# Attention and mixture of experts on one core: weight loads one step earlier, beta added batch by batch, packing of experts in four parts

## The chip, the cores and the metric

The kernel runs on one core of a Trainium2 chip. The metric is the device time of one execution in microseconds (us). Engines are named as the profile does: PE is TensorE, DVE is VectorE, ACT is ScalarE, POOL is GpSimd, SP is SyncE, which here only issues transfers.

## The reference

The input is x, 32 batches of 256 tokens of 128 numbers. Everything is float32.

```
xn  = layernorm(x)                                   # without gamma and beta
out = x + attention(xn) + experts(xn)

attention(t): q, k, v = split(t @ w_qkv), 16 heads of 8
              a = softmax(causal(q k^T / sqrt(8))) v
              layernorm(a @ w_proj + b_proj + t) * gamma + beta
experts(t):   p = softmax(t @ Wr^T), 8 experts, the best 2 of each token
              sum over those: p_e * (gelu(t @ W1[e] + b1[e]) @ W2[e] + b2[e])
```

## The kernel before

All of the work is written out by engine; an engine runs its own list in order, and semaphores tie the lists together. There are four stages.

1. x is loaded and normalised; the router's logits are computed, and each token gets two places (slots) among the rows of its experts.
2. A loop of steps does the attention. In step s batch s is projected to q and k (PROJECT), the row maxima of batch s-1 are found (MAXIMA), batch s-2 goes through scores and exponentials (SOFT), batch s-3 through the rest up to the projection and the statistics of the second layernorm (FINISH), and batch s-4 gets gamma and is added to the residual (LAST). The list `USES` sets, for all engines, the order of the pieces of work inside a step: m0 to m11 are the products whose maxima VectorE takes (L1192 and L1196 on TensorE, L966 on VectorE), s0 to s5 the scores (L1178, L1182) with their exponentials on ScalarE (L687) and causal masks on POOL (L601), o0 and o1 the products with v (L1213), then transposes (oT, onT), the projection (proj) and the transposed maxima (shift). Steps 1 to 3 and 24 to 35 are written out; between them most engines run a loop with two steps in its body. POOL's steps are all written out.
3. Experts: 72 tiles of 256 slots, each gathered, multiplied with the two matrices of its expert and scattered.
4. The two results of each token are added to the residual and stored.

What the change touches stands in the second stage:

- **Weights of the experts.** W1 and W2 come in eight pieces of 512 KB through two buffers. SP loads piece i with `load_piece` (L424); ScalarE copies it to float16 (`high_piece`, L691, behind the copy of v, L704), and VectorE stores the difference (`low_piece`, L1036, behind the statistics of proj, L993 to L1002). `pieces(s)` says which piece a step splits: pieces 0 to 6 in steps 24 to 30, piece 7 in step 32. Pieces 0 and 1 are loaded before the loop. Piece i from 2 on is loaded at the start of the step that splits it, ahead of that step's store of q and k (L460) in SP's queue; the loads of q and k by heads (L446, L447) and of the maxima (L481) follow.
- **Beta.** `add_beta` on POOL (L579) adds beta to the residual x_all, eight tiles of 128 tokens in one instruction. Tiles 0 to 31 are done before the loop, the others in steps 5, 7, 9 and 11.
- **Order on POOL in a step.** Indirect sends of normalised rows to their slots (`send_tile`, L592, two DMAs per tile; two tiles in a step, from step 24 on three in every even one), then add_beta where the step has one, then the mask of s0, the add of the normed batch to x_all (`add_normed`, L607), a power (L613), the residual with the bias (L621), and the masks of s1 to s5.
- **Gamma.** `last` on VectorE (L1009), a pair of instructions per step, behind the maximum m11.
- **Packing of experts.** `pack_experts` on VectorE (L939 to L953), 16 operations each waiting for the one before, finds the expert of each tile and packs the numbers for the loops of stage 3. It stands at the end of step 3 (FINISH), behind proj's statistics and ahead of the next step's m0.

## Time and profile before

| | |
|---|---|
| median of 3 runs | 832.76 us (831.69 to 836.01) |
| the profiled execution | 832.92 us, of which 831.2 are the span |
| mean granted clock | 0.953 |
| PE busy | 695.6 us, 84% of the span |
| DVE busy | 663.3 us, 80% |
| ACT busy | 548.3 us, 66% |
| POOL busy | 552.3 us, 66% |
| chain that ended last | PE 65%, DVE 11%, DMA 7%, ACT 7%, issue 4%, SP's queue 3%, POOL 2% |

The span is from the first to the last instruction. The granted clock is TensorE's, as a share of 2.4 GHz; its other level is 1.2 GHz. An engine is busy while an instruction of it runs; the share of the whole span is a mean over the four stages. A row of a timeline has the start in us from the span's start, the duration in us (with "x5", from the start of the first to the end of the last of five merged ones), the engine, the line, the operation, out<-in, shapes, and in brackets the idle time before it with what ended it.

### The profile page before, as it was taken

What the parts mean: (1) busy time and instruction counts of PE and PEld (TensorE: products, weight loads), DVE (VectorE), ACT (ScalarE), POOL (GpSimd) and SP (SyncE); (2) the same over time, 40 slices, a digit from 0 to 9 for tenths busy, and PEclk for the clock granted to TensorE, in tenths of its full rate; (3) what the DMA queues carried; (4) which work ended last, traced back from release to release, by engine and by line L of the source; (5) the groups of instructions that cost most, each with busy time, mean ns of one, the idle gap of its engine ahead of it and who ended that gap; (6) DMA issues with size and microseconds to landing.
All of it is one profiled execution on the core that took longest, in us unless ns stands there. A gap on an engine that the chain in (4) does not pass through costs nothing.

```text
span 831.2 us, 24989 instructions
## 1 busy us (share of the span) xinstructions
PE 695.6 (84%) x7877; PEld 516.5 (62%) x7878; DVE 663.3 (80%) x1550; ACT 548.3 (66%) x1107; POOL 552.3 (66%) x611
## 2 busy tenths in 40 slices
PE   2766989898899999999878888669999999999800
PEld 1543656565666666666656555338988889888700
DVE  5878988889898898989988886537888888888644
ACT  4812656666576767767667665538989999999700
POOL 8522768877787888878768676616666667667700
PEclk9998999999999999999999999859999999999955
DMA  9692223232323232333253342102222222222189
GB/s 263 241 304 70 92 82 99 84 102 84 103 82 110 93 104 92 108 105 96 81 158 110 104 135 65 29 13 77 89 81 87 80 87 85 83 78 89 51 276 336
DMA packets 113313, 93.66 MB, mean 113 GB/s; under 512 B 16618, under 2 KB 97650, under 8 KB 113268
## 3 DMA queue, kind: packets, MB, share of 16 engines
q1 hardware_dynamic: 95508, 70.26, 27.4%
q0 software_dynamic: 8704, 18.17, 6.1%
q10 hardware_dynamic: 9056, 4.66, 1.9%
q8 instruction: 25, 0.41, 0.2%
q14 instruction: 20, 0.16, 0.1%
HBM read 43.85 MB, written 48.93 MB: 112 GB/s over the span
## 4 chain that ended last, share of the span: by engine, by line
PE 65%; DVE 11%; DMA 7%; ACT 7%; issue 4%; SPq 3%; POOL 2%; ACTq 0%; POOLq 0%; DVEq 0%
PE wide L1324 11%; PE bank_head L1213 7%; PE wide L1178 6%; PE bank_head L1315 5%; PE bank_maxB L1315 5%; PE bank_maxA L1192 5%; PE bank_maxB L1192 4%; DMA xn_rows<-parts_dram 3%; PE bank_misc L1238 3%; DMA pieces_f<-in_w 3%; PE wide L1182 3%; PE bank_maxB L1196 3%; PE bank_maxA L1196 3%; DVE y L1009 2%; SPq L481 2%
## 5 line engine op out<-in xcount | busy, mean ns | idle before, releaser
L653 POOL DMA_INDIRECT parts_dram<-o_T,dest x144 | 160.5, 1115 | 76.6 <-issue 47.9
L687 ACT ACTIVATE probs<-wide 128x1024 f32<-128x1024 f32 x192 | 188.7, 1021 | 32.8 <-PE wide L1178 19.2
L601 POOL TENSOR_SCALAR_AFFINE_SELECT probs<-probs 128x512 f32<-128x512 f32 (+1 forms) x192 | 152.2, 804 | 83.9 <-ACT probs L687 83.1
L592 POOL DMA_INDIRECT x_slots<-xn_rows,slot_i x128 | 127.1, 993 | 37.6 <-issue 36.5
L966 DVE TENSOR_REDUCE shift<-bank_maxA 128x2 f32<-128x512 f32 (+1 forms) x192 | 132.2, 689 | 13.8 <-PE bank_maxA L1196 10.1
L966 DVE TENSOR_REDUCE shift<-bank_maxB 128x2 f32<-128x512 f32 (+1 forms) x192 | 131.7, 686 | 7.8 <-PE bank_maxB L1196 4.1
L731 ACT ACTIVATE probs<-wide,b_all 128x256 f32<-128x256 f32 x288 | 121.2, 477 | 16.9 <-PE wide L1324 11.0
L1324 PE MATMUL wide<-xgT_raw,xnT 128*128 128x256 f16 x864 | 109.2, 277 | 6.6 <-DVE xgT_raw L1074 6.6
L1057 DVE TENSOR_TENSOR probs<-probs 128x512 f16<-128x512 f32 x144 | 99.8, 693 | 5.4 <-ACT probs L737 1.1
L1213 PE MATMUL bank_head<-probs,v_aug 128*32 128x256 f32 (+1 forms) x2048 | 98.8, 334 | 6.4 <-POOL probs L601 6.3
L1192 PE MATMUL bank_maxA<-k_cat,q_diag 128*128 128x128 f16 (+1 forms) x512 | 76.0, 251 | 19.5 <-DVE shift L966 17.9
L1324 PEld LDWEIGHTS wide<-xgT_raw,xnT 128*128 x864 | 78.7, 99 | 19.4 <-issue 7.6
L1213 PEld LDWEIGHTS bank_head<-probs,v_aug 128*32 128x32 f32 x2048 | 59.3, 111 | 49.5 <-issue 16.8
L1178 PE MATMUL wide<-q_diag,k_cat 128*128 128x512 f16 x256 | 77.5, 386 | 3.3 <-DMA q_diag<-shift_T 3.0
L1192 PE MATMUL bank_maxB<-k_cat,q_diag 128*128 128x256 f16 (+1 forms) x512 | 75.5, 251 | 0.5 <-DVE shift L966 0.2
L711 ACT ACTIVATE o_T<-bank_head 128x512 f32<-128x512 f32 x64 | 38.2, 597 | 54.5 <-PE bank_head L1213 52.0
L1192 PEld LDWEIGHTS bank_maxA<-k_cat,q_diag 128*128 128x128 f16 x512 | 38.7, 98 | 45.5 <-DVE shift L966 31.9
L1192 PEld LDWEIGHTS bank_maxB<-k_cat,q_diag 128*128 128x128 f16 x512 | 42.9, 99 | 31.2 <-DVE shift L966 11.0
L1196 PE MATMUL bank_maxA<-mask,ident 128*128 128x256 f16 (+1 forms) x192 | 60.4, 314 | 0.0
L1196 PE MATMUL bank_maxB<-mask,ident 128*128 128x256 f16 (+1 forms) x192 | 60.3, 314 | 0.0
L1315 PE MATMUL bank_head<-xnT,probs 128*128 x864 | 56.1, 222 | 0.0
L1315 PE MATMUL bank_maxB<-xnT,probs 128*128 x864 | 55.1, 220 | 0.2 <-DVE probs L1057 0.2
(178 smaller groups left out, 1263.9 us busy)
## 6 DMA issues: line engine op xcount, KB each, us to landing
qk_rows<-split SPq DMA_DIRECT2D x32, 512.0 KB
x_slots<-fill SPq DMA_DIRECT2D x16, 598.5 KB, 7.7
fill<-x_slots SPq DMA_DIRECT2D x72, 133.0 KB
q_diag<-qk_rows SPq DMA_DIRECT2D x256, 32.0 KB, 1.8
k_cat<-qk_rows SPq DMA_DIRECT2D x64, 128.0 KB, 2.1
xn_rows<-parts_dram SPq DMA_DIRECT2D x8, 1024.0 KB, 11.7
x_all<-in_x SPq DMA_DIRECT2D x8, 512.0 KB, 8.2
pieces_f<-in_w SPq DMA_DIRECT2D x8, 512.0 KB, 4.3
```

The lines of the kernel that those rows point to most:

```text
L592: pool.indirect_dma_start(out=x_slots, out_offset=bass.IndirectOffsetOnAxis(ap=slot_i[:, t, c:c + 1], axis=0), in_=xn_rows[:, t, :], in_of ...
L601: pool.affine_select(out=part, in_=part, compare_op=ALU.is_ge, fill=0.0, base=0, pattern=[[0, n], [1, P]], channel_multiplier=-1).then_inc ...
L653: pool.indirect_dma_start(out=parts_dram, out_offset=bass.IndirectOffsetOnAxis(ap=dest[:, of, t:t + 1].bitcast(U32), axis=0), in_=y[:, of ...
L687: act.activation(probs[:, u, :], ps[:, :], ACT.Exp, scale=SCALE).then_inc(empty, 1)
L731: act.activation(hT[:, par, c, :], wide[par][:, S * c:S * (c + 1)], ACT.Gelu, bias=b1_all[:, bass.ds(e, 1), c:c + 1].rearrange("p a b -> p ...
L966: V.tensor_reduce(dst, ps[:, :].rearrange("p (j k) -> p j k", j=nh), axis=AX.X, op=ALU.max, negate=True).then_inc(empty, 1)
L1178: last = M(ps[:, 512 * h2:512 * (h2 + 1)], keys[:, gs[0], :], q_diag[:, par, gs[0], 2 * h2:2 * h2 + 2, :], start=True, stop=True)
L1192: M(ps[:, keys * n_:keys * (n_ + 1)], q_diag[:, 1 - par, g, j, P * qt:P * (qt + 1)], k_cat[:, 1 - par, g, 0:keys], start=(n_ == 0), stop=F ...
L1196: M(dst, ident16[:, :], mask16[:, :].rearrange("p (o k) -> p o k", o=1).to_broadcast([P, nh, P]), start=False, stop=True, skip_group_check ...
L1213: last = M(dst, v_aug[:, of, kt, J * g + j, :], p_, start=(kt == 0), stop=(kt == 1), skip_group_check=True)
L1315: last = M(results[:, D * t:D * (t + 1)], hT_parts[:, par, hp, c, P * t:P * (t + 1)], w2_parts[:, wp_, bass.ds(e_2, 1), c, :].rearrange("p ...
L1324: last = M(wide[par][:, S * c:S * (c + 1)], w1_parts[:, wp_, bass.ds(e_1, 1), P * c:P * (c + 1)].rearrange("p a d -> p (a d)"), xgT[:, par ...
```

## The change

Three edits, with one more that one of them needs.

SP loads piece i+1 at the start of the step that splits piece i, from piece 1 on, after a wait for the split of piece i-1, whose buffer it takes. Piece 7 thus goes out in step 30. `add_beta` takes a first tile and a number of tiles; before the loop nothing changes, and in the loop one batch (two tiles) is added in each of steps 5 to 20. `pack_experts` has four parts, at the ends of steps 4, 5, 6 and 7: the three operations that find the experts, then four, four and two of the ten packing operations, and with the last part the three closing ones. As these steps differ, VectorE's loop begins with step 8 instead of step 4, and steps 4 to 7 are written out for it.

```diff
-        def steps(eng, step, after=((), ()), first_tile=None, written_out=False):
+        def steps(eng, step, after=((), ()), first_tile=None, written_out=False, in_loop=STAGES - 1):
...
-            first_whole = STAGES - 1 if not written_out else TAIL
+            first_whole = in_loop if not written_out else TAIL
...
                 for i in pieces(s):
-                    if i >= 2:
-                        sp.wait_ge(piece_low, i - 1)
-                        load_piece(i)
+                    if 1 <= i < PIECES - 1:
+                        sp.wait_ge(piece_low, i)
+                        load_piece(i + 1)
...
-            def add_beta(c):
-                tiles_ = slice(NT // BETA_PARTS * c, NT // BETA_PARTS * (c + 1))
-                pool.tensor_tensor(x_all[:, tiles_, :], x_all[:, tiles_, :],
-                                   beta_bc[:, :].rearrange("p (o d) -> p o d", o=1).to_broadcast([P, NT // BETA_PARTS, D]),
-                                   ALU.add).then_inc(res_ready if c == BETA_PARTS // 2 - 1 else offset_ready, 1)
+            def add_beta(begin, count):
+                mine = x_all[:, begin:begin + count, :]
+                pool.tensor_tensor(mine, mine, beta_bc[:, :].rearrange("p (o d) -> p o d", o=1).to_broadcast([P, count, D]),
+                                   ALU.add).then_inc(res_ready if begin + count == NT // 2 else offset_ready, 1)
...
-                    if what == "m0" and s in (5, 7, 9, 11):
-                        add_beta(BETA_PARTS // 2 + (s - 5) // 2)
+                    if what == "m0" and 5 <= s < 5 + B // 2:
+                        add_beta(QT * (B // 2 + s - 5), QT)
...
-            def pack_experts():
-
-                dve.wait_ge(slots_filled, 256)
-                then_pack(V.tensor_tensor(past[:, :, :], tile_start[:, :].rearrange("p (t o) -> p t o", o=1).to_broadcast([P, NS, E]),
-                                     over_tiles(ends[:, :], NS), ALU.is_ge))
-                then_pack(V.tensor_reduce(expert[:, :], past[:, :, :], axis=AX.X, op=ALU.add))
-                then_pack(V.tensor_scalar(padded_experts[:, 2:2 + NS], expert[:, :], float(E - 1), None, ALU.min))
-                for j in range(FIELDS):
+            def pack_experts(part):
+
+                if part == 0:
+                    dve.wait_ge(slots_filled, 256)
+                    then_pack(V.tensor_tensor(past[:, :, :], tile_start[:, :].rearrange("p (t o) -> p t o", o=1).to_broadcast([P, NS, E]),
+                                              over_tiles(ends[:, :], NS), ALU.is_ge))
+                    then_pack(V.tensor_reduce(expert[:, :], past[:, :, :], axis=AX.X, op=ALU.add))
+                    then_pack(V.tensor_scalar(padded_experts[:, 2:2 + NS], expert[:, :], float(E - 1), None, ALU.min))
+                for j in (range(0, 0), range(0, 4), range(4, 8), range(8, FIELDS))[part]:
...
+                if part == 3:
+                    then_pack(V.tensor_copy(packed_i[:, :, :], packed[:, :, :]))
...
-                if isinstance(s, int) and s == FINISH:
-                    pack_experts()
+                if isinstance(s, int) and FINISH < s <= FINISH + 4:
+                    pack_experts(s - FINISH - 1)
...
-            steps(dve, step, after=((), (places,)), first_tile=lambda: tile(0, 0, None))
+            steps(dve, step, in_loop=FINISH + 5, after=((), (places,)), first_tile=lambda: tile(0, 0, None))
```

How it moves the work shows in the lists of three engines. In the changed kernel the lines below L311 of the file are off by one here and there (L592 is L591, L1002 is L1003).

SP, from the end of step 24 to the start of step 26, before (L424 is the load of a piece, L460 the store of q and k):

```order
L481 DMA q_diag<-shift_T 1x4x256 x4
L460 DMA qk_rows<-split 128x2x1024
L446 DMA q_diag<-qk_rows 32x2x256 x4
L447 DMA k_cat<-qk_rows 128x2x256
L446 DMA q_diag<-qk_rows 32x2x256 x4
L447 DMA k_cat<-qk_rows 128x2x256
L481 DMA q_diag<-shift_T 1x4x256 x4
L424 DMA pieces_f<-in_w 128x2x512
L460 DMA qk_rows<-split 128x2x1024
```

and in the changed kernel:

```order
L481 DMA q_diag<-shift_T 1x4x256 x4
L424 DMA pieces_f<-in_w 128x2x512
L460 DMA qk_rows<-split 128x2x1024
L446 DMA q_diag<-qk_rows 32x2x256 x4
L447 DMA k_cat<-qk_rows 128x2x256
L446 DMA q_diag<-qk_rows 32x2x256 x4
L447 DMA k_cat<-qk_rows 128x2x256
L481 DMA q_diag<-shift_T 1x4x256 x4
L424 DMA pieces_f<-in_w 128x2x512
```

The load of piece 2 now stands in front of step 25's store of q and k instead of step 26's, and each later load has moved in the same way.

POOL, step 5 and the sends of step 6, before (L579 adds beta, L607 the normed batch):

```order
L592 DMA x_slots<-xn_rows,slot_i 18432x133 x4
L579 TENSOR_TENSOR x_all<-x_all,beta_bc 128x1024
L601 AFFINE_SELECT probs<-probs 128x4x128
L607 TENSOR_TENSOR x_all<-x_all,y2 128x256
L613 TENSOR_TENSOR rstd2<-mv2,half 128x2
L621 TENSOR_TENSOR xpb<-xn_rows,bproj_bc 128x256
L601 AFFINE_SELECT probs<-probs 128x4x128
L601 AFFINE_SELECT probs<-probs 128x1024
L601 AFFINE_SELECT probs<-probs 128x4x128 x2
L601 AFFINE_SELECT probs<-probs 128x1024
L592 DMA x_slots<-xn_rows,slot_i 18432x133 x4
L601 AFFINE_SELECT probs<-probs 128x4x128
```

and in the changed kernel, from the last masks of step 5:

```order
L600 AFFINE_SELECT probs<-probs 128x4x128 x2
L600 AFFINE_SELECT probs<-probs 128x1024
L591 DMA x_slots<-xn_rows,slot_i 18432x133 x4
L579 TENSOR_TENSOR x_all<-x_all,beta_bc 128x256
L600 AFFINE_SELECT probs<-probs 128x4x128
L606 TENSOR_TENSOR x_all<-x_all,y2 128x256
```

The add is a quarter of its size and now stands behind the sends of step 6 too, and so on to step 20.

VectorE, where the packing stood, from the end of step 3 to the loop, before (L1002 closes the statistics, L939 begins the packing):

```order
L1002 TENSOR_SCALAR mv<-mv 128x2
L939 TENSOR_TENSOR fill<-tile_start,ends 128x576
L941 TENSOR_REDUCE expert<-fill 128x72
L942 TENSOR_SCALAR padded_experts<-expert 128x72
L947 COPY packed<-padded_experts 128x10
L949 SCALAR_TENSOR_TENSOR packed<-padded_experts,packed 128x10 x4
L947 COPY packed<-padded_experts 128x10
L949 SCALAR_TENSOR_TENSOR packed<-padded_experts,packed 128x10 x4
L951 CAST packed_i<-packed 128x20
L952 TENSOR_SCALAR packed_i<-packed_i 128x10
L953 TENSOR_TENSOR packed_i<-packed_i 128x10
```

and in the changed kernel, the end of step 4 and the start of step 5 (L967 takes the maxima, L983 splits q and k):

```order
L1010 SCALAR_TENSOR_TENSOR y<-x,mv,gamma_bc 128x128 x2
L994 TENSOR_TENSOR x<-bank_misc,xpb 128x256
L997 BN_STATS st<-x 128x6 x2
L1001 BN_AGGR mv<-st 128x2 x2
L1003 TENSOR_SCALAR mv<-mv 128x2
L939 TENSOR_TENSOR fill<-tile_start,ends 128x576
L941 TENSOR_REDUCE expert<-fill 128x72
L942 TENSOR_SCALAR padded_experts<-expert 128x72
L967 TENSOR_REDUCE shift<-bank_maxA 128x4
L967 TENSOR_REDUCE shift<-bank_maxB 128x2
L983 TENSOR_TENSOR split<-bank_misc,split 128x2x256
```

Three of the sixteen operations are left at one place, a step later than before; the other thirteen follow the statistics of steps 5, 6 and 7.

## Rows read from the trace of the kernel before

**Rows 1.** Stretches: us from:to, length, busy time of each engine (instructions), granted clock, DMA share, GB/s.

```profile
90.11:106.77 16.66, 14.63 (x171) 9.36 (x159) 14.67 (x40) 9.33 (x13) 12.66 (x15) 1.00 0.29 93
106.77:121.33 14.56, 14.28 (x134) 9.12 (x137) 11.72 (x27) 8.83 (x13) 8.09 (x11) 0.88 0.23 75
121.33:149.97 28.64, 27.09 (x304) 17.80 (x296) 24.27 (x52) 18.76 (x28) 23.53 (x28) 1.00 0.31 98
149.97:224.19 74.22, 66.99 (x748) 44.86 (x740) 66.23 (x131) 46.95 (x70) 61.35 (x70) 1.00 0.28 91
237.51:370.84 133.33, 133.20 (x1488) 89.00 (x1480) 118.41 (x260) 93.17 (x140) 106.55 (x131) 1.00 0.31 100
384.05:400.66 16.61, 13.92 (x169) 9.45 (x158) 15.55 (x28) 10.27 (x15) 14.30 (x17) 1.00 0.33 99
400.66:414.25 13.59, 13.14 (x152) 8.95 (x148) 12.82 (x28) 10.26 (x15) 9.64 (x11) 1.00 0.28 89
414.25:493.81 79.56, 67.11 (x748) 45.51 (x741) 66.53 (x137) 51.25 (x75) 60.34 (x72) 1.00 0.40 124
107.20:110.60 3.40, 3.21 (x18) 1.73 (x16) 2.35 (x5) 0.96 (x2) 0.25 (x1) 0.65 0.47 174
514.10:518.10 4.00, 3.98 (x19) 2.83 (x20) 1.94 (x4) 2.25 (x3) 3.90 (x6) 0.57 0.00 0
```

**Rows 2.** Timeline of VectorE, the packing and the maximum behind it.

```profile
100.81 0.75 DVE L939 TENSOR_TENSOR fill<-tile_start,ends 128x576 f32<-128x576 f32 x1
...
102.62 0.17 DVE L947 COPY packed<-padded_experts 128x10 f32<-128x10 f32 x1
...
105.57 0.69 DVE L966 TENSOR_REDUCE shift<-bank_maxA 128x4 f32<-128x512 f32 x1 [0.25 <-DVE packed_i L953]
```

**Rows 3.** Timeline of TensorE, the first product of step 4 that waits.

```profile
106.32 0.39 PE L1192 MATMUL bank_maxA<-k_cat,q_diag 128*128 128x256 f16 x2 [1.90 <-DVE shift L966]
```

**Rows 4.** Timelines of VectorE and TensorE, the split in step 25 and step 26's wait.

```profile
411.92 1.21 DVE L1036 TENSOR_TENSOR xnT<-pieces_f,xnT 128x1024 f16<-128x1024 f32 x1
...
415.78 0.39 PE L1192 MATMUL bank_maxA<-k_cat,q_diag 128*128 128x256 f16 x2 [0.20 <-DVE shift L966]
```

**Rows 5.** Timeline of POOL in step 23, a clean one.

```profile
373.07 0.96 POOL L592 DMA_INDIRECT x_slots<-xn_rows,slot_i  x1 [0.30 <-issue]
374.88 0.63 POOL L601 TENSOR_SCALAR_AFFINE_SELECT probs<-probs 128x512 f32<-128x512 f32 x1 [0.86 <-ACT probs L687]
375.49 0.71 POOL L607 TENSOR_TENSOR x_all<-x_all,y 128x256 f32<-128x256 f32 x1
...
380.22 0.73 POOL L601 TENSOR_SCALAR_AFFINE_SELECT probs<-probs 128x512 f32<-128x512 f32 x1 [0.28 <-ACT probs L687]
```

**Rows 6.** Timeline of POOL in step 7: the add of beta and the masks.

```profile
153.18 2.38 POOL L579 TENSOR_TENSOR x_all<-x_all,beta_bc 128x1024 f32<-128x1024 f32 x1
...
158.17 3.93 POOL L601 TENSOR_SCALAR_AFFINE_SELECT probs<-probs 128x512 f32<-128x512 f32 x5
```

**Rows 7.** Timeline of VectorE, the gamma pair in steps 7, 23 and 24.

```profile
158.98 3.27 DVE L1009 SCALAR_TENSOR_TENSOR y<-x,mv,gamma_bc 128x128 f32<-128x128 f32 x2
...
379.85 0.60 DVE L1009 SCALAR_TENSOR_TENSOR y<-x,mv,gamma_bc 128x128 f32<-128x128 f32 x2
...
393.07 3.71 DVE L1009 SCALAR_TENSOR_TENSOR y<-x,mv,gamma_bc 128x128 f32<-128x128 f32 x2
```

**Rows 8.** Waits: who waited for what, us in total, times, longest.

```profile
ACT xnT L691 <- DMA pieces_f<-in_w: 16.4, 6, 3.6
```

**Rows 9.** DMA issues: number, KB each, median us from issue to landing.

```profile
pieces_f<-in_w SPq DMA_DIRECT2D x8, 512.0 KB, 4.3
```

**Rows 10.** Timeline of POOL, masks of step 24 and first send of step 26.

```profile
392.49 3.88 POOL L601 TENSOR_SCALAR_AFFINE_SELECT probs<-probs 128x512 f32<-128x512 f32 x5
...
412.16 1.88 POOL L592 DMA_INDIRECT x_slots<-xn_rows,slot_i  x1 [0.17 <-issue]
```

**Rows 11.** Timeline of TensorE in step 32.

```profile
514.12 0.80 PE L1182 MATMUL wide<-q_diag,k_cat 128*128 128x512 f16 x2 [2.51 <-ACT probs L687]
```

More of the change, by code:

```diff
@@ L587, in _ @@
             for c in range(BETA_PARTS // 2):
-                add_beta(c)
+                add_beta(NT // BETA_PARTS * c, NT // BETA_PARTS)
             def send_tile(t):
@@ L950, in pack_experts @@
                                                     op0=ALU.mult, op1=ALU.add))
-                then_pack(V.tensor_copy(packed_i[:, :, :], packed[:, :, :]))
-                then_pack(V.tensor_scalar(packed_i[:, 1, :], packed_i[:, 1, :], BITS * FIELDS // 2, None, ALU.logical_shift_left))
-                then_pack(V.tensor_tensor(packed_i[:, 0, :], packed_i[:, 0, :], packed_i[:, 1, :], ALU.bitwise_or))
-                assert packing_count == EXPERTS_PACKED, packing_count
+                if part == 3:
+                    then_pack(V.tensor_copy(packed_i[:, :, :], packed[:, :, :]))
+                    then_pack(V.tensor_scalar(packed_i[:, 1, :], packed_i[:, 1, :], BITS * FIELDS // 2, None, ALU.logical_shift_left))
+                    then_pack(V.tensor_tensor(packed_i[:, 0, :], packed_i[:, 0, :], packed_i[:, 1, :], ALU.bitwise_or))
+                    assert packing_count == EXPERTS_PACKED, packing_count
             FAR = 1e38
@@ L1127, in _ @@
             picks()
-            steps(dve, step, after=((), (places,)), first_tile=lambda: tile(0, 0, None))
+            steps(dve, step, in_loop=FINISH + 5, after=((), (places,)), first_tile=lambda: tile(0, 0, None))
             tiles(dve, tile, load=False, begun=1)
             dve.wait_ge(res_ready, B + 1)
-            dve.wait_ge(offset_ready, BETA_PARTS - 1)
+            dve.wait_ge(offset_ready, BETA_PARTS // 2 - 1 + B // 2)
             for c in range(LAST_CHUNKS):
```

## The prediction

> **What bounds the kernel now.** I read the stretches first, cut at the starts of VectorE's split of q and k (L982), so that each is whole steps of the loop [rows 1]. Steps 13 to 22 take 133.33 us, 13.33 each, and TensorE is busy for 133.20 of them at clock 1.00: a clean step is TensorE's own work, and no edit to another engine makes it shorter. What a step takes beyond 13.33 is a wait, and that is all this change can win. The same rows show where such steps are: 3 (16.66), 4 (14.56), 5 and 6 (28.64), 7 to 11 (74.22), 24 (16.61), 26 to 30 (79.56). Steps 3 to 11 are 14.1 over nine clean ones, steps 26 to 30 12.9 over five. Then I read each engine's timeline at those places to see which wait ends last, and the list of waits for ScalarE's on the weights.
>
> **Packing of experts.** Before, the 16 small operations stand at the end of step 3. They start at 100.81, and the next maximum at 105.57 [rows 2]: some 4.5 us of VectorE, after which TensorE has waited 1.90 us for that maximum [rows 3]. Then the granted clock is 0.65 over the next 3.4 us, so part of it at 1.2 GHz, with TensorE busy for 3.21 [rows 1]. Together steps 3 and 4 are 3.33 + 1.23 = 4.56 over. Without the packing I let them keep 0.4 for the other small waits of a young pipeline, so 4.15 goes.
>
> It comes back in four parts. The first three operations took 102.62 - 100.81 = 1.81 [rows 2] and now end step 4; the other 2.7 (105.57 - 102.62, less 0.25 idle) are three parts of some 0.9 at the ends of steps 5, 6 and 7. The trace of before has no such part in a clean step. The nearest row is the split of a weight piece, 1.21 us at the same place of a step: TensorE then waits 0.20 for a maximum [rows 4]. So about 1.0 at that place is hidden by VectorE's slack against TensorE. Parts of 0.9 cost nothing, 1.81 costs 0.8; I add 0.1 for the last. Bounds: 0, and 4.5 if no slack were there. Net for the packing: 4.15 - 0.9 = **3.25 gained**.
>
> **Beta.** Before, POOL adds it to eight tiles at a time in steps 5, 7, 9 and 11. In a clean step POOL's last send ends at 374.03 and the first mask starts at 374.88, after 0.86 idle, waiting for ScalarE's exponential; later there is a pause of 0.28 before the fourth of the other masks [rows 5]. In step 7 the add (2.38) fills that idle time and some 1.5 more: POOL is late, its five masks run from 158.17 with no pause [rows 6]. In that time VectorE wants to multiply by gamma (L1009). In the clean step its pair takes 0.60; here 3.27, from 158.98 to 162.25, as long as the masks run [rows 7]. So this pair, whose two inputs are both in SBUF, gets in only when POOL pauses, and TensorE then waits for what is behind it. The cost is read off the steps: 28.64 - 26.66 = 1.98 for steps 5 and 6, 74.22 - 66.65 = 7.57 for 7 to 11 (three adds, 2.52 each), 9.55 in all.
>
> The new add has two tiles (128x256), in each of steps 5 to 20, right behind the fourth indirect send. It is not in the trace of before; between 0.6 and 2.38 us is what POOL's additions take. I take 0.71: the add of the normed batch has its very shape and takes that [rows 5]. It fits into the 0.86 with 0.15 left, so the mask starts when it did. Sixteen adds are 11.4 us of POOL instead of four times 2.38 = 9.5, all under that idle time. Were that cover gone, 0.28 of pause is left, and beyond it a step costs 2.52 as in step 7. **9.55 gained**; the bounds are this and the second rival.
>
> **Weight pieces.** ScalarE waits 16.4 us for them, in six steps, 3.6 at most [rows 8]: a load lands 4.3 us after its issue [rows 9], and before it is issued at the start of the step that needs it. A step earlier it has 13 us. What SP now waits for before a load is the split of the piece before last, in the step before; such a split ends at 413.1 (411.92 + 1.21), before the next step's start at 414.25 [rows 1, 4], so SP passes. Behind that wait in SP's queue stands the store of q and k, for which the next step's maxima wait.
>
> But in steps 26 to 30 something is late next. From step 24 on, every even step issues six indirect sends instead of four, and POOL is late there too. ScalarE's wait hides that, since the masks then wait for late exponentials. What is under it stands in steps 24 and 25, whose pieces were loaded long before: step 24 has five masks without a pause (3.88) [rows 10] and the gamma pair takes 3.71 [rows 7]; it is 16.61 long, and step 25, with four sends, 13.59 [rows 1]. So I put 16.61 for steps 26, 28, 30 and 13.59 for 27 and 29: 77.0 instead of 79.56, **2.55 gained**, out of 12.8 us of waiting that vanish there. Bounds: all five at 13.59 gives 11.6; a first send of 1.88, as step 26 has it behind a split that began earlier [rows 4, 10], instead of 0.96 [rows 5], in each even step gives 2.8 back, so a little below 0.
>
> The last piece is needed in step 32. There TensorE waits 2.51 for ScalarE [rows 11], and in the next 4.0 us the clock is 0.57 with TensorE busy throughout [rows 1]. At full clock that work is 4.0 x 0.57 = 2.3 if all of it goes with the clock; I take 2.5, 1.5 less. Of these 4.0 I keep 0.2 back: **3.8 gained**; bounds 0 and 4.2. The later stages (expert tiles, last additions) start earlier and are as long as before.
>
> **Sum.** 3.25 + 9.55 + 2.55 + 3.8 = 19.15 from the profiled execution's 832.92 us: **813.8 us**. The median of the runs, 832.76, is 0.16 below that execution, so nothing is corrected.
>
> **Rivals.**
>
> *Port (B).* Here a rule speaks against the change. The rows show one direction, VectorE's pair held off by POOL [rows 7], and perhaps the other: a first send of 1.88 behind a split that began 0.24 earlier [rows 4, 10]. Ten of the packing's operations have two inputs in SBUF, and they now stand in four steps beside POOL's last mask and first sends. If they hold POOL up by more than the 0.15 + 0.28 left, the masks close up in steps 5 to 8 and the gamma pair is caught again: 4 x 2.52 = 10.1, so 823.9. For it: the 1.88. Against it: these operations are short, and in step 5 the maxima, hence the exponentials, come later by the same 0.8. I give it 0.12. The Trainium skill, "SBUF — State Buffer", Who interferes with whom, says that a VectorE instruction with two SBUF inputs contends with a GpSimd instruction that reads SBUF, and that the first to start holds the shared ports for its whole length while the other is blocked. The 3.27 beside 0.60 agrees, though five masks went by and not one; by that rule alone the time would be 823.9, by the trace's slack 813.8.
>
> *POOL too full (C), the other side.* If the small add costs more than 0.86 + 0.28 = 1.14, POOL is late in each of steps 5 to 20 that begins without extra room; the step after a caught one has it again (as step 8 has after 7), so eight of sixteen are caught: 8 x 2.52 = 20.2, that is 834.0, 1.1 slower than before and within noise; with B on top 844, plainly slower. For it: the margin is only 0.15, and adds are four times as many. Against it: the same shape at 0.71 [rows 5]. 0.08 (0.05 for 834, 0.03 for 844).
>
> *Early loads change nothing (D).* POOL's sends, or the transfers that now crowd the start of a step (DMA share 0.40 in steps 26 to 30 against 0.28 in step 25 [rows 1]), take the place of the load wait everywhere; also if the load is still issued late because SP stands at another wait. Then 2.55 + 3.8 fall away: 820.2. Chance 0.08.
>
> *Even steps freed (E).* If steps 26, 28 and 30 fall to 13.59 as well, 9.05 more goes: 804.8. Against it stands step 24, which has no load wait and is 16.61. 0.04.
>
> **How the numbers follow.** My case has 0.68. Its own range is 810 to 818: the packing's 0.9 between 0 and 3, the even steps 1.5 either way, and 1.5 for where the low-clock stretches fall. The range must take in B and D and may leave out C and E: 809 to 824. A measurement here can tell about 0.5% (4.2 us) from no change. Faster by more: A, B, D, E, 0.92; within: 834, 0.05; slower: 844, 0.03.
>
> **What would show it.** Right: no step from 7 to 22 over 13.5; the gamma pair at 0.6 in all of them; POOL's add at about 0.7 with 0.1 to 0.2 idle before the next mask; TensorE's 1.90 wait gone and no low clock near 107 us; no ScalarE wait on the pieces; steps 26, 28 and 30 still near 16.6 with masks that don't pause. Wrong: the gamma pair long in steps 5 to 20 (B or C); a ScalarE wait for a piece, or a late first half of q (D); even steps under 15 (E).

## The result and the profile after

The changed kernel takes **812.59 us** (median of 4 runs, 810.48 to 814.95) against 832.86 for the kernel before on the same chip: ratio 0.975, 95% interval 0.971 to 0.979. The forecast was 813.8. The profiled execution took 811.8 us, span 810.1, against 832.92 and 831.2. The total is right; as the experiments show, its division among the terms of the sum is not.

Stretches of the changed kernel, cut as [rows 1] at VectorE's split of q and k (now L983), columns as there: steps 3; 4; 5 and 6; 7 to 11; 13 to 22; 24; 25; 26 to 30; step 31 to the end.

```profile
91.14:104.74 13.60, 13.57 (x158) 8.89 (x151) 10.86 (x24) 8.74 (x12) 10.35 (x13) 1.00 0.33 104
104.74:119.11 14.37, 14.36 (x167) 9.41 (x159) 13.30 (x29) 9.70 (x15) 10.86 (x13) 1.00 0.30 95
119.11:146.68 27.57, 26.36 (x286) 17.31 (x289) 24.52 (x61) 18.27 (x28) 22.32 (x28) 1.00 0.30 97
146.68:213.34 66.66, 66.53 (x744) 44.48 (x740) 59.68 (x137) 46.63 (x70) 57.05 (x71) 1.00 0.31 99
226.66:360.33 133.67, 133.16 (x1488) 89.10 (x1480) 118.41 (x260) 93.24 (x140) 112.65 (x139) 1.00 0.31 100
373.54:390.15 16.61, 13.91 (x169) 9.44 (x157) 15.55 (x28) 10.28 (x15) 14.30 (x17) 1.00 0.32 99
390.15:403.75 13.60, 13.15 (x152) 8.95 (x148) 12.83 (x29) 10.27 (x15) 9.65 (x11) 1.00 0.41 128
403.75:481.41 77.66, 66.47 (x748) 45.54 (x741) 73.16 (x137) 51.38 (x75) 62.79 (x73) 1.00 0.41 128
481.41:810.10 328.69, 260.17 (x3264) 227.48 (x3260) 239.68 (x599) 239.81 (x621) 191.88 (x182) 0.92 0.33 102
```

Steps 7 to 11 are clean (66.66 for 74.22), step 3 is (13.60 for 16.66), steps 24 and 25 are what they were, and steps 26 to 30 fell by 1.90. Of the 21.1 us that the span lost, 11.9 went in steps 3 to 11, 1.9 in steps 26 to 30, and 8.7 behind the start of step 31 (337.39 to 328.69); steps 1 and 2 gave back 1.0 and step 15 0.44.

POOL's timeline in step 8 shows beta's new addition (L579):

```profile
163.08 0.75 POOL L579 TENSOR_TENSOR x_all<-x_all,beta_bc 128x256 f32<-128x256 f32 x1
164.10 0.64 POOL L600 TENSOR_SCALAR_AFFINE_SELECT probs<-probs 128x512 f32<-128x512 f32 x1 [0.27 <-ACT probs L686]
...
169.43 0.73 POOL L600 TENSOR_SCALAR_AFFINE_SELECT probs<-probs 128x512 f32<-128x512 f32 x1 [0.28 <-ACT probs L686]
170.48 1.09 POOL L600 TENSOR_SCALAR_AFFINE_SELECT probs<-probs 128x1024 f32<-128x1024 f32 x1 [0.32 <-ACT probs L686]
```

It takes 0.73 to 0.75 in all sixteen steps. In step 8 the pauses of 0.28 and 0.32 before the last two masks are still there, and VectorE's gamma pair slips into the first:

```profile
169.06 0.60 DVE L1010 SCALAR_TENSOR_TENSOR y<-x,mv,gamma_bc 128x128 f32<-128x128 f32 x2
```

In step 15 the addition does not fit. The first mask follows it at once, the next masks come later, and the gamma pair takes 1.17:

```profile
256.52 0.74 POOL L579 TENSOR_TENSOR x_all<-x_all,beta_bc 128x256 f32<-128x256 f32 x1
257.33 0.64 POOL L600 TENSOR_SCALAR_AFFINE_SELECT probs<-probs 128x512 f32<-128x512 f32 x1
...
262.29 1.17 DVE L1010 SCALAR_TENSOR_TENSOR y<-x,mv,gamma_bc 128x128 f32<-128x128 f32 x2
```

The step takes 13.76 for 13.32. This belongs to beta: step 15 is 13.72 to 13.77 in every run that has an addition there, whatever its size, and 13.32 to 13.35 in every run that has none.

ScalarE's wait for the pieces [rows 8] is gone altogether. TensorE's wait of 1.90 [rows 3] is gone too.

### The profile page after: what moved, and what is told of

It is laid out like the page before. It is cut to its first block, busy times and chain, and to the rows that moved or that the text cites. A ratio compares the mean times of both kernels' runs of the same rounds, so it can differ in the third digit from the quotient of the medians.

```text
span 810.1 us, 24948 instructions
## 1 busy us (share of the span) xinstructions
PE 688.6 (85%) x7877; PEld 512.9 (63%) x7878; DVE 661.2 (82%) x1550; ACT 548.4 (68%) x1107; POOL 557.4 (69%) x623
## 4 chain that ended last, share of the span: by engine, by line
PE 68%; DVE 13%; ACT 5%; DMA 5%; issue 4%; SPq 2%; POOL 2%; ACTq 0%; POOLq 0%; DVEq 0%
PE wide L1325 11%; PE bank_head L1214 7%; PE wide L1179 7%; PE bank_head L1316 6%; PE bank_maxA L1193 5%; PE bank_maxB L1316 5%; PE bank_maxB L1193 5%; PE bank_misc L1239 3%; DMA xn_rows<-parts_dram 3%; DVE shift L967 3%; PE wide L1183 3%; PE bank_maxA L1197 3%; PE bank_maxB L1197 3%; DVE y L1010 2%; PE bank_misc L1222 2%
## 5 line engine op out<-in xcount | busy, mean ns | idle before, releaser
L591 POOL DMA_INDIRECT x_slots<-xn_rows,slot_i x128 | 129.2, 1009 | 37.4 <-issue 35.5
L967 DVE TENSOR_REDUCE shift<-bank_maxA 128x2 f32<-128x512 f32 (+1 forms) x192 | 132.1, 688 | 12.9 <-PE bank_maxA L1197 9.1
L967 DVE TENSOR_REDUCE shift<-bank_maxB 128x2 f32<-128x512 f32 (+1 forms) x192 | 131.5, 685 | 7.5 <-PE bank_maxB L1197 3.6
L730 ACT ACTIVATE probs<-wide,b_all 128x256 f32<-128x256 f32 x288 | 121.4, 478 | 16.6 <-PE wide L1325 10.8
L1325 PE MATMUL wide<-xgT_raw,xnT 128*128 128x256 f16 x864 | 107.9, 275 | 6.8 <-DVE xgT_raw L1075 6.8
L1214 PE MATMUL bank_head<-probs,v_aug 128*32 128x256 f32 (+1 forms) x2048 | 96.5, 329 | 8.4 <-POOL probs L600 8.4
L1214 PEld LDWEIGHTS bank_head<-probs,v_aug 128*32 128x32 f32 x2048 | 58.1, 109 | 50.3 <-issue 19.9
L1179 PE MATMUL wide<-q_diag,k_cat 128*128 128x512 f16 x256 | 76.8, 383 | 3.8 <-DMA q_diag<-shift_T 3.8
L1316 PE MATMUL bank_head<-xnT,probs 128*128 x864 | 55.5, 220 | 0.0
## 6 DMA issues: line engine op xcount, KB each, us to landing
xn_rows<-parts_dram SPq DMA_DIRECT2D x8, 1024.0 KB, 11.7
```

What stands on the lines that cost most here:

```text
L591: pool.indirect_dma_start(out=x_slots, out_offset=bass.IndirectOffsetOnAxis(ap=slot_i[:, t, c:c + 1], axis=0), in_=xn_rows[:, t, :], in_of ...
L730: act.activation(hT[:, par, c, :], wide[par][:, S * c:S * (c + 1)], ACT.Gelu, bias=b1_all[:, bass.ds(e, 1), c:c + 1].rearrange("p a b -> p ...
L967: V.tensor_reduce(dst, ps[:, :].rearrange("p (j k) -> p j k", j=nh), axis=AX.X, op=ALU.max, negate=True).then_inc(empty, 1)
L1179: last = M(ps[:, 512 * h2:512 * (h2 + 1)], keys[:, gs[0], :], q_diag[:, par, gs[0], 2 * h2:2 * h2 + 2, :], start=True, stop=True)
L1214: last = M(dst, v_aug[:, of, kt, J * g + j, :], p_, start=(kt == 0), stop=(kt == 1), skip_group_check=True)
L1316: last = M(results[:, D * t:D * (t + 1)], hT_parts[:, par, hp, c, P * t:P * (t + 1)], w2_parts[:, wp_, bass.ds(e_2, 1), c, :].rearrange("p ...
```

## The experiments

The first question is which part earned what. I put each part alone into the kernel before, and profiled both kernels once more.

**Beta alone.** The edit is the fourth and fifth piece of the diff, of which the fifth is shown:

```diff
...
-                    if what == "m0" and s in (5, 7, 9, 11):
-                        add_beta(BETA_PARTS // 2 + (s - 5) // 2)
+                    if what == "m0" and 5 <= s < 5 + B // 2:
+                        add_beta(QT * (B // 2 + s - 5), QT)
```

> The kernel before with the new beta alone (two tiles in each of steps 5 to 20); packing in step 3 and late loads stay. Theory (POOL's additions under 1.14 us are free, longer ones let one pair of gamma be caught): 832.8 - 9.55 = 823.3; steps 3 and 4 stay at 16.7 and 14.6, steps 5 to 11 fall from 102.9 to 93.5, steps 26 to 30 stay at 79.6, gamma pair 0.6 in steps 5 to 23. Rival (part of the fall in steps 5 to 11 came from the packing, which no longer starts them late): under 8 us, 825 to 829. Rival (additions four times as many fill POOL): 833 or more.

Measured: 826.96 us (821.71 to 832.27, 8 runs), ratio 0.992, interval 0.9885 to 0.9955, or 6.7 us with 3.8 to 9.6. The median lies in the range of the first rival, 825 to 829. Steps 5 to 11 took 95.0, against 102.9 and, in the second profile below, 102.6; nearly all of the fall is in steps 7 to 11, and steps 5 and 6 stayed at 28.3.

**Packing alone.**

```diff
...
-                if isinstance(s, int) and s == FINISH:
-                    pack_experts()
+                if isinstance(s, int) and FINISH < s <= FINISH + 4:
+                    pack_experts(s - FINISH - 1)
```

> The kernel before with the packing spread over steps 4 to 7 alone. Theory: 832.8 - 3.25 = 829.5; steps 3 and 4 fall from 31.2 to 28.0, and up to 1 us of it is given back in steps 5 and 6; the wait of 1.90 us and the low clock near 107 us are gone. Rival (the give-back is larger, since the parts now stand in the steps with the long additions to which they add): steps 5 to 8 longer by 1 to 3 us, 831 to 833.

Measured: 832.3 us (826.89 to 837.75, 12 runs), ratio 0.9969, interval 0.9939 to 0.9998: 2.6 us, with 0.2 to 5.1. Steps 3 and 4 took 28.05, as forecast, and the wait of 1.90 us is gone. Steps 5 to 8, which the rival makes 1 to 3 us longer, took 57.2, against 57.8 and 57.6 in the two profiles of the kernel before.

**Early loads alone.**

```diff
-                    if i >= 2:
-                        sp.wait_ge(piece_low, i - 1)
-                        load_piece(i)
+                    if 1 <= i < PIECES - 1:
+                        sp.wait_ge(piece_low, i)
+                        load_piece(i + 1)
```

> The kernel before with loads one step ahead alone. Theory as predicted: steps 26 to 30 fall by 2 to 2.6, step 32 by 3.8 to 4.2: 832.8 - 6.4 = 826.4, and the first expert tile's stretch stays as it was (products of 2.5 to 2.8 us at half clock). Second theory (the short low-clock stretch after step 32 that the changed kernel has follows from step 32 without its stall): 4.2 more, 822.2, with those products at 1.5. Rival (that stretch falls by chance or by when the earlier steps end): 826.4, with no sameness to the changed kernel. Rival (early loads change nothing): 832.8.

Measured: 822.46 us (821.2 to 823.33, 5 runs), ratio 0.9866, interval 0.9837 to 0.9896: 11.2 us, with 8.7 to 13.6. That is nearly twice the 6.35 forecast, which lies outside the interval. The second theory's 822.2 is met, but not by its mechanism: TensorE is at half clock for 20.5 us between the start of step 31 and 560 us, not for the 10.2 of the changed kernel. Steps 26 to 30, then step 31 to the end:

```profile
413.96:490.76 76.80, 67.24 (x761) 45.72 (x751) 71.53 (x137) 51.33 (x75) 61.39 (x73) 1.00 0.43 130
490.76:820.20 329.44, 263.66 (x3264) 229.78 (x3260) 240.01 (x599) 240.03 (x621) 191.88 (x182) 0.91 0.33 102
```

The three ratios give 6.7 + 2.6 + 11.2 = 20.5, and the whole change 20.3 to 20.7: within the intervals, some 4.5 us on the sum, the parts add up.

**Both kernels once more**, without an edit.

> The kernel before once more, for its trace alone. If the low-clock stretch between 533 and 561 us belongs to that kernel, the time from the start of step 31 to the end is again 337 us; if it fell badly by chance in that execution, 334 as in the two kernels that keep the late loads; the steps 26 to 30 differ from 79.6 by as much as the loads land earlier or later.

> The changed kernel once more, timed on the same chip as the run beside it. If the end of 328.7 us from the start of step 31 on belongs to that kernel, it is 328 to 330 again and the median 812 to 813; if the low clock fell well by chance in the execution profiled, 331 to 334 and 814 to 816. Its spread stays at half of the 11 us of the kernel before, since no load is waited for.

Measured: 834.06 (one run) and 813.37 us (5 runs, 813.12 to 814.53; ratio 0.9758). The end of the kernel before was 334.0, so its 337.4 had been bad luck; that of the changed kernel was 330.8, so a part of its 328.7 had been good luck. Lengths in us, all cut at the split of q and k:

| execution | steps 3 to 6 | 7 to 11 | 26 to 30 | 31 to end |
|---|---|---|---|---|
| before | 59.9 | 74.2 | 79.6 | 337.4 |
| before, again | 58.1 | 74.2 | 85.5 | 334.0 |
| beta alone | 58.0 | 66.7 | 82.6 | 334.6 |
| packing alone | 56.0 | 74.3 | 86.1 | 334.1 |
| early loads alone | 58.1 | 74.2 | 76.8 | 329.4 |
| after | 55.5 | 66.7 | 77.7 | 328.7 |
| after, again | 56.3 | 66.7 | 76.5 | 330.8 |

Down the columns: steps 7 to 11 belong to beta, to 0.1 us. Steps 3 to 6 belong to the packing: 58.5 in the mean without it, 55.9 with it. Steps 26 to 30 and the end belong to the early loads: 83.4 against 77.0, and 335.0 against 329.6.

The same stretches show why one execution misled me. Of the kernel before, again, steps 3; 4; 5 and 6; 26 to 30 (cut to 0.1 us, so up to 0.1 from the table):

```profile
90.50:107.30 16.80, 14.71 (x171) 9.41 (x163) 14.70 (x41) 9.33 (x13) 12.75 (x15) 1.00 0.31 97
107.30:120.20 12.90, 12.62 (x134) 8.44 (x137) 11.69 (x27) 8.72 (x13) 7.99 (x11) 1.00 0.25 81
120.20:148.70 28.50, 27.02 (x304) 17.71 (x299) 23.73 (x53) 18.64 (x28) 23.66 (x28) 1.00 0.31 100
...
412.80:498.32 85.52, 71.56 (x748) 48.39 (x740) 65.69 (x136) 51.15 (x75) 61.43 (x71) 0.94 0.37 115
```

In step 4 the clock is 1.00 and the step 12.90, where [rows 1] has 0.88 and 14.56. TensorE waited the same 1.90 us before it in both [rows 3], here

```profile
106.83 0.39 PE L1192 MATMUL bank_maxA<-k_cat,q_diag 128*128 128x256 f16 x2 [1.90 <-DVE shift L966]
```

With beta alone and with early loads alone, which keep the packing where it was, the step is 12.95. So the low clock there was that execution's own, not the packing's. Steps 5 and 6 are as long as with the small additions (28.3 in the run of beta alone), so the first large addition, in step 5, cost next to nothing; what else lengthens these two steps stays open. And steps 26 to 30 took 6 us more, with clock 0.94. ScalarE's wait for the pieces, of the kernel before, again, and of the packing alone:

```profile
ACT xnT L691 <- DMA pieces_f<-in_w: 19.3, 6, 4.1
```

```profile
ACT xnT L691 <- DMA pieces_f<-in_w: 20.1, 6, 4.3
```

Beside 16.4 and 3.6 [rows 8], the first profile had caught a cheap draw. The spread of the times agrees in part: 11.1 us over the 19 runs of the kernel before in this comparison and 10.6 over 8 with beta alone, but 2.1 over 5 with early loads alone. The changed kernel has 4.5 over 4 and 1.4 over 5, and four runs of the kernel before also had no more than 4.3, so the number of runs has a share in it.

**What room POOL has.** The rival C of the prediction decides at an addition of 1.14 us. I put beta in four tiles into every second step.

```diff
-                    if what == "m0" and 5 <= s < 5 + B // 2:
-                        add_beta(QT * (B // 2 + s - 5), QT)
+                    if what == "m0" and s in range(5, 5 + B // 2, 2):
+                        add_beta(QT * (B // 2 + s - 5), 2 * QT)
...
```

> The changed kernel with the same beta in four tiles in every second step, 5 to 19, eight additions instead of sixteen. Between 0.73 us for two tiles and 2.38 for eight, four would take 1.28, which is 0.14 over POOL's room of 0.86 + 0.28 = 1.14. Theory (beyond the room the masks run without a pause and the gamma pair waits until they end, so the full price falls due at once): gamma pair above 3 in all eight steps, each of them 15.8 instead of 13.3, 812.6 + 20 = 832. Rival (the price grows with how late POOL is): 0.3 a step, 815. Rival (POOL's lateness costs nothing by itself): 812.6 or a little under.

Measured: 815.73 us (815.27 to 818.41, 4 runs; ratio 0.9786, interval 0.9737 to 0.9835, beside 0.9752 and 0.9758 for the changed kernel). The 2 to 3 us more are within the noise of the times; the steps show them. Those from 9 to 19 that carry an addition take 13.72 to 13.75, with the gamma pair at 1.15 to 1.16. POOL and then VectorE in step 9:

```profile
176.28 1.29 POOL L579 TENSOR_TENSOR x_all<-x_all,beta_bc 128x512 f32<-128x512 f32 x1
177.50 0.65 POOL L600 TENSOR_SCALAR_AFFINE_SELECT probs<-probs 128x512 f32<-128x512 f32 x1
...
180.18 2.90 POOL L600 TENSOR_SCALAR_AFFINE_SELECT probs<-probs 128x512 f32<-128x512 f32 x4
183.50 1.09 POOL L600 TENSOR_SCALAR_AFFINE_SELECT probs<-probs 128x1024 f32<-128x1024 f32 x1 [0.41 <-ACT probs L686]
```

```profile
182.08 1.15 DVE L1010 SCALAR_TENSOR_TENSOR y<-x,mv,gamma_bc 128x128 f32<-128x128 f32 x2
```

The pause before the fourth of the other masks is gone, as forecast, but not the one before the fifth, and the pair is done there. My full price at 1.14 falls: beyond it a step costs 0.4. By the same reckoning there is a second threshold at 1.14 + 0.32 = 1.46, beyond which the pair waits until the last mask ends and a step costs 2.5. That one is not measured: no run has an addition between 1.29 and 2.38.

Nor is a pause the only way in. In step 7 of the kernel before, where the masks run on without one [rows 6], the pair's first operation and the masks around its end are

```profile
158.98 1.59 DVE L1009 SCALAR_TENSOR_TENSOR y<-x,mv,gamma_bc 128x128 f32<-128x128 f32 x1
159.80 0.62 POOL L601 TENSOR_SCALAR_AFFINE_SELECT probs<-probs 128x512 f32<-128x512 f32 x1
160.39 0.67 POOL L601 TENSOR_SCALAR_AFFINE_SELECT probs<-probs 128x512 f32<-128x512 f32 x1
```

so it ends while the fourth mask is under way; only the second operation waits for the last.

**Why even steps are long.** Six sends make POOL late, the gamma pair is held off for 3.7 to 4.4 us, and TensorE waits. Is it the pair's wait that costs, or that the masks themselves are late? Here POOL waits after its second mask until the pair is done.

```diff
...
                         mask(s, int(what[1:]))
+                        if what == "s1" and s >= TAIL and s % 2 == 0 and has(s, LAST):
+                            pool.wait_ge(y2_ready, (s - LAST) * QT + QT + 1)
```

> The changed kernel, where in the even steps from 24 on POOL waits after its second mask until the gamma pair of that step is done; six sends stay. Theory (VectorE's pair is held off for as long as masks follow one another, and TensorE waits for what stands behind the pair): the pair falls from 3.7 to 4.4 to about 1 (it begins while a mask runs), POOL ends its masks about 0.6 later, VectorE about 2.5 earlier; steps 24, 26, 28, 30 fall from 16.6 to 16.9 to about 14.3: 812.6 - 10 = 803. Rival (the price is POOL's own lateness: the products wait for masks that come late): another 0.6 late in each, 815. In between if both hold: the gain is what is left above the wait for the last mask.

Measured: 816.28 us (813.37 to 820.01, 6 runs; ratio 0.9787, interval 0.9745 to 0.9828), nothing gained. The pair takes 0.61 in step 24 and 0.98 to 1.00 in 26, 28 and 30. Step 24 falls from 16.61 to 15.05, step 26 to 15.04, but steps 28 and 30 are 17.04 and 16.61, and steps 25, 27 and 29 grow to 14.1 to 14.4; in all, steps 24 to 30 take 106.6, where the two profiles of the changed kernel have 107.9 and 106.7. What TensorE waits for in step 24 now:

```profile
385.26 1.51 PE L1216 MATMUL bank_head<-probs,v_aug 128*32 128x256 f32 x32 [1.77 <-POOL probs L600]
```

So neither side holds alone. The pair's wait is a part of the price, and POOL's own lateness another: freeing the pair turns a wait for VectorE into a longer one for the masks. The changed kernel has both in step 24:

```profile
383.79 1.51 PE L1214 MATMUL bank_head<-probs,v_aug 128*32 128x256 f32 x32 [1.01 <-POOL probs L600]
386.98 0.38 PE L1247 MATMUL bank_misc<-ident,shift 128*16 128x128 f32 x2 [1.68 <-DVE x L994]
```

The second profile of the changed kernel shows the same without an edit. In its step 28 five masks run without a pause, the gamma pair gets in between them and takes 1.25, and the step takes 15.03, where the first profile has 3.76 and 16.89:

```profile
443.25 3.99 POOL L600 TENSOR_SCALAR_AFFINE_SELECT probs<-probs 128x512 f32<-128x512 f32 x5
444.45 1.25 DVE L1010 SCALAR_TENSOR_TENSOR y<-x,mv,gamma_bc 128x128 f32<-128x128 f32 x2
```

The masks begin 8.7 us after the start of the step in both profiles. So of the 3.3 us that step 28 has over a clean step in the first, 1.9 come from the pair's wait, and 1.4 are left for POOL's lateness. Why the pair gets in there, and in step 24 of both profiles not, stays open.

**Fewer sends at once.** If POOL's lateness costs, sends have to be dealt out. First evenly, five in each step from 24 on:

```diff
...
-                places = ("m0", "m0", "m0") if (s - TAIL) % 2 == 0 else SEND_AFTER
-                begin = 2 * (TAIL - SEND) + (5 * (s - TAIL) + 1) // 2
...
+            begin, count = (4 * (s - SEND), 4) if s < TAIL else (4 * (TAIL - SEND) + 5 * (s - TAIL), 5)
...
```

> The changed kernel with five indirect sends in each step from 24 on (4 in the last) instead of six and four by turns; same count, same last step. Theory (a send of 0.96 more behind the four is under POOL's 1.14 of room, two are over it, and over it the gamma pair is caught): steps 24, 26, 28, 30 fall from 16.6 to 16.9 each to 13.4 to 13.7, about 12.5 us: 800. Rival (first sends stretched to 1.9 beside the weight's split use up the room): half of the steps caught whichever way they are dealt, 812 or up to 3 less. Rival (the even steps are long for another reason than POOL's lateness, such as the scattered writes themselves, which are as many): 812.6.

Measured: 810.71 us (806.94 to 813.57, 6 runs; ratio 0.9721, interval 0.9687 to 0.9755), 2 to 3 under the changed kernel, within the noise, where 12.5 was expected. Steps 24 to 30 took 100.3 instead of 107.9 or 106.7. Steps 24, 26 and 28 are 14.1 to 14.5 with the pair at 1.15 to 1.57, and step 29 is 16.74. I had counted a send as 0.96, but POOL also stands 0.30 at "issue" before each, so a fifth takes 1.26, over the first threshold; but these steps cost 0.7 to 1.1 over the 13.4 of step 25, not 0.4, and I did not find what makes up the rest. In step 29 POOL began the fifth 2.52 after the end of the fourth:

```profile
446.99 0.96 POOL L585 DMA_INDIRECT x_slots<-xn_rows,slot_i  x1 [0.31 <-issue]
450.47 0.96 POOL L585 DMA_INDIRECT x_slots<-xn_rows,slot_i  x1 [2.52 <-ACT probs L680]
```

That is not this run's own. It is the 114th of the 128 sends, and in all twelve traces the 114th, whatever its place in step 29, comes 0.74 to 3.27 after the one before it, where every other send that follows a send comes 0.30 or 0.31 after it. What it waits for stays open. In the second profile of the changed kernel it is 3.27, and step 29 takes 17.39. The end lost 5.2 us against the first profile of the changed kernel and 3.1 against the second (333.9), with a fifth send now in step 31 and 23.8 us at half clock there instead of 10.2 and 17.0; I did not part these two.

Then early: the eight sends over four a step go to steps 5 to 12, and beta behind the loop.

```diff
...
+            begin, count = 4 * (s - SEND) + min(max(s - 5, 0), 8), 5 if 5 <= s < 13 else 4
...
             steps(pool, step, written_out=True)
+            pool.wait_ge(res_ready, B + 1)
+            for b in range(B // 2, B):
+                add_beta(QT * b, QT)
```

> The changed kernel with beta's second half added behind the step loop, in the gap before the expert tiles, and the eight sends that are over four a step dealt one each to steps 5 to 12; steps 24 to 32 have four. Theory (0.96 of one more send fits into the room of 1.14 as 0.73 did): steps 5 to 12 as in the changed kernel, steps 24 to 30 between 13.3 and 13.7, 107.9 down to about 95, additions in the gap free: 812.6 - 12.5 = 800. Rival (a fifth send is too much): every second of steps 5 to 12 caught, 10 given back, 810. Rival (the split of a weight piece alone makes POOL late, by stretching the first send to 1.9): steps 24 to 30 stay above 14.5 on average, 806 or more.

Measured: 805.15 us (803.72 to 806.48, 6 runs; ratio 0.965, interval 0.9613 to 0.9686). Steps 26 to 30, then step 31 to the end:

```profile
400.90:468.88 67.98, 66.27 (x740) 44.82 (x740) 63.54 (x137) 50.79 (x75) 57.49 (x65) 1.00 0.45 138
468.88:802.30 333.42, 265.19 (x3272) 230.01 (x3264) 245.04 (x599) 239.69 (x621) 206.48 (x200) 0.91 0.33 101
```

TensorE is now busy for 66.27 of 67.98 there, and step 31 begins 12.5 us earlier than in the first profile of the changed kernel, 11.7 earlier than in the second. So the last rival fails: the first send is 1.88 in steps 25 to 31, and these steps are still 13.4 to 14.0. Of the eight steps with a fifth send, 7, 9 and 11 cost 0.4 to 0.5 more (9 and 11 are 13.75, the pair 1.18): 1.26 is over 1.14, as the first threshold says, and the step behind a delayed one has room again. But the end is 4.7 longer than in the first profile of the changed kernel and 2.6 longer than in the second. To see whether the additions in the gap do that, beta went back into the loop, in three tiles a step:

```diff
...
+                    if what == "m0" and 13 <= s < 24:
+                        add_beta(NT // 2 + 3 * (s - 13), min(3, NT // 2 - 3 * (s - 13)))
...
```

> The changed kernel with the eight extra sends dealt to steps 5 to 12 as in the run before, but beta's second half back in the loop: three tiles in each of steps 13 to 22 and two in step 23. From 0.73 for two tiles, 1.29 for four, three take 1.0. Theory as it now stands (POOL's room is 0.86 of idle time and two pauses of 0.28 and 0.32: up to 1.14 nothing is lost, up to 1.46 the pair waits for the second pause and a step costs 0.4, beyond it waits for the last mask and costs 2.5): steps 13 to 23 stay at 13.3, steps 5 to 12 as in the run before (three of 13.75), the start of step 31 near 469; with the end as long as the changed kernel's (329) 799 to 800, with the end as in the run before (333) 804. Rival (any addition over 0.86 costs 0.4): five or six of the eleven steps at 13.7, 2 more.

Measured: **802.92 us** (801.22 to 804.94, 5 runs; ratio 0.9635, interval 0.9605 to 0.9665), beside 813.37 for the changed kernel on the same chip: it beats both kernels and lies within the forecast. Step 31 begins at 471.28 and the end is 328.2; the 10.2 us at half clock there, as in the first profile of the changed kernel, differ between executions, so it is not shown that the additions in the gap made the end longer. The addition of three tiles takes 1.01 to 1.02, and of steps 13 to 23 nine stay at 13.2 to 13.4; step 15 takes 13.73, as it does with additions of two and of four tiles, and step 19 13.59. That speaks for the room of 1.14 and against the rival's five or six steps at 13.7.

## Why the prediction was right

**Bound by waits, clean steps untouched: right but for one.** Steps 13 to 22 are 133.67 instead of 133.33; step 15 alone, which beta's addition makes late, is 0.44 of that. The sign "no step from 7 to 22 over 13.5" fails there, and in step 7 with 13.75, which carries the packing's last part (step 8 is 12.95 for it).

**Packing, 3.25: about 2.6.** The mechanism held: step 3 is clean, the wait of 1.90 is gone, and the first part lengthens step 4. But that costs 1.4 (14.37 instead of 12.9 to 12.95), where 0.8 was put. And step 4's 1.23 should not have been charged to the packing; that was a stretch of low clock of one execution, absent in the three others that have the packing at its old place.

**Beta, 9.55: about 7.6.** Three additions of 2.52, 7.57, are right to 0.1. The 1.98 for steps 5 and 6 were not beta's. That the small addition just fits is right in fifteen of sixteen steps (0.73 to 0.75 for 0.71). That the pair "gets in only when POOL pauses" is not: its first operation got in between two masks in step 7 already.

**Pieces in steps 26 to 30, 2.55: 6.4 on the mean of the executions**, though 1.9 between the two that I compared. The forecast of what the steps become, 77.0, is right (77.7, 76.5, 76.8). What failed is the other side, "79.56", taken as the kernel's while it is one draw of 79.6 to 86.1. The even steps did stay near 16.6 in the first profile: 16.88, which goes with the stretched first send that I had named as a bound (1.88 at 401.65). In the second only the sum is met: steps 28, 29 and 30 are 15.03, 17.39 and 13.60.

**Step 32 and the end, 3.8: 5.4 on the means, 8.7 between the two executions.** The stall is gone and step 32 gave 4.2. Its low clock is gone too: the four executions with late loads have a stretch at half clock 20.4 to 20.6 us behind the start of step 31, and those with early loads have none within 28 us of it. I held the later stages to be as long as before. They are not: where the pipeline empties, TensorE has gaps and falls to half clock for stretches that differ by execution, two of them in the kernel before (534.9 to 545.1 and 548.5 to 562.2), one after (529.8 to 540.0), and two again in the second profile of the changed kernel (521.8 to 525.2 and 528.6 to 542.2). What decides where they fall stays open.

So 2.0 too much for beta and 0.6 for the packing stand against 3.9 too little for the pieces in the loop and 1.6 at the end; steps 1, 2 and 15 took back 1.4 between the two first profiles. A right sum with wrong terms is partly luck.

**Rivals.** B did not come: no pair is caught in steps 5 to 8. The first of the packing's parts begins at 116.10 and a send beside it takes 1.42 instead of 0.96, so it does touch POOL, but POOL had the time, and the 10.1 us that I worked out for B were not lost:

```profile
116.10 0.75 DVE L939 TENSOR_TENSOR fill<-tile_start,ends 128x576 f32<-128x576 f32 x1
116.34 1.42 POOL L591 DMA_INDIRECT x_slots<-xn_rows,slot_i  x1 [0.17 <-issue]
```

The send ends 0.91 after the VectorE operation, and so does the one of 1.88 behind the split of a weight piece (401.41 + 1.21 = 402.62, 401.65 + 1.88 = 403.53). In the twelve traces 85 sends begin during an operation of these two kinds, and all end 0.83 to 0.91 after it. So the send waits for the operation's end. The Trainium skill ("SBUF — State Buffer", Who interferes with whom) says that the first to start holds the shared ports while the other is blocked, and the stretched sends agree; the same section has it that a `tensor_tensor` does not stall such transfers, for a reason that it calls inferred, and there these rows, of sends whose offsets (slot_i) also lie in SBUF, do not agree. C did not come, and its deciding point was wrong: at 1.29 an addition costs 0.4, not 2.52. D is refuted by the early loads alone. E, against which step 24 spoke, did not come in the sum (76.5 to 77.7, not 68), but it is what fewer sends bring: 68.0.

## What to carry to other kernels

A stretch whose length hangs on a load that is waited for, or on the clock behind a stall, is a draw: take a second profile of the same kernel before a difference of a few us is booked to one part, and see whether the spread of the runs fits. Moving a load ahead of its need may also narrow the spread; here the numbers of runs are too unlike to show by how much. An engine's room is the sum of its pauses in order, and what lies beyond one pause need not cost what lies beyond the next: here 0.4 beyond the first, and 2.5 where all were gone. An operation takes up its pitch, the issue gap included, and not its duration alone.

## What the runs showed of the hardware

A pair of VectorE operations with two SBUF inputs took up to 4.89 us instead of 0.60 beside POOL masks that followed one another, its first operation waiting across up to five of them. It got in at pauses of 0.28 us or more, and sometimes between two masks without one (step 7 of the kernel before; step 28 of the second profile of the changed kernel, 1.25), but not always.

In the other direction, an indirect send on POOL that began during a VectorE operation with two SBUF inputs ended 0.83 to 0.91 us after that operation, in 85 of 85 cases, so it took up to 1.98 instead of 0.96. Sends in a row came at a pitch of 1.26 us.

The 114th of 128 indirect sends came 0.74 to 3.27 us after the one before it in each of twelve traces, wherever it stood; the cause is open.

The loads of the weight pieces took 4.3 to 4.8 us in the median in the four executions that waited for them, yet what ScalarE waited went from 16.4 to 20.1 in all. In steps 26 to 30 of the kernel before the granted clock was 1.00 in one execution and 0.94 in another.
